# Routed experts of a two-layer network: token rows gathered three groups ahead, target work moved one round later, and eight constant products added to each round

## The reference, cut to what matters

```python
buf = jnp.zeros((E, CAPACITY + 1, H), x.dtype).at[e_flat, slot].set(x[tok])   # E = 64, CAPACITY = 64, H = 128
gu_e = jnp.einsum('ech,ehf->ecf', buf, expert_gate_up_w)
act = _silu(gu_e[..., :I]) * gu_e[..., I:]                                     # I = 64
out_e = jnp.einsum('eci,eih->ech', act, expert_down_w)
y = out_e[e_flat, slot] * w_flat[:, None]
y = jnp.where((pos < CAPACITY)[:, None], y, 0)
y = y.reshape(T, TOP_K, H).sum(axis=1)
```

## Time and profile before

| | before |
|---|---|
| times of 3 runs | 1703.34, 1703.63 (median), 1709.86 us |
| the profiled execution: its time, its span | 1707.66 us, 1704.8 us |
| busy of the span: PE, DVE, ACT, POOL | 88%, 66%, 58%, 54% |
| mean granted clock of TensorE, share of full | 0.941 |
| expert stage: first gather to the end of the span | 1555.9 to 1704.8 us |

### The profile page before, as it was taken

The page is one execution under the profiler, slowest core; times in us unless marked ns, Lnnn a source line. Parts: engine busy times, 40 slices in busy tenths (PEclk is TensorE's granted clock), DMA queues, the critical chain, the costliest instruction groups (busy, mean ns, idle before and its releaser), DMA issues.

```text
span 1704.8 us, 44671 instructions
## 1 busy us (share of the span) xinstructions
PE 1504.1 (88%) x13893; PEld 1081.1 (63%) x13895; DVE 1131.8 (66%) x2702; ACT 989.5 (58%) x2495; POOL 926.9 (54%) x1633
## 2 busy tenths in 40 slices
PE   7989999999999999997999688888888888885786
PEld 5545555555555555545999577777777777774675
DVE  6566555555555555552555598998898998895662
ACT  6445555555555555542334588888888888872342
POOL 6235555555555545545543566666666666632664
PEclk8789999999999999998999699999999999996775
DMA  9132131222222221213332121211211211215442
GB/s 278 36 83 56 48 78 50 55 54 55 57 57 57 57 57 46 54 52 78 65 70 61 28 49 44 46 41 42 46 43 41 45 43 41 45 38 113 87 91 36
DMA packets 240850, 103.36 MB, mean 61 GB/s; under 512 B 145497, under 2 KB 229274, under 8 KB 240794
## 3 DMA queue, kind: packets, MB, share of 16 engines
q1 hardware_dynamic: 230554, 89.04, 22.4%
q0 software_dynamic: 10240, 13.64, 3.7%
HBM read 57.73 MB, written 35.96 MB: 55 GB/s over the span
## 4 chain that ended last, share of the span: by engine, by line
PE 44%; ACT 15%; DMA 11%; DVE 10%; SPq 9%; issue 7%; POOL 4%; POOLq 0%; DVEq 0%; ACTq 0%
DMA remainders<-yT 5%; PE bankA L1883 4%; PE bankB L1929 4%; PE bankT L1912 4%; PE bankT L2068 4%; SPq L370 4%; DMA dq<-remainders 3%; DVE mneg L998 3%; ACT qx L1688 3%; ACT km L1697 2%; ACT gqx L1688 2%; PE bankT L2187 2%; PE bankS L1897 2%; PE bankA L2169 2%; ACT rows L1761 2%
## 5 line engine op out<-in xcount | busy, mean ns | idle before, releaser
L683 POOL TENSOR_SCALAR_AFFINE_SELECT probs<-probs 128x512 f32<-128x512 f32 x256 | 183.4, 739 | 175.0 <-ACT probs L1574 175.0
L1574 ACT ACTIVATE probs<-bankT 128x1024 f32<-128x1024 f32 x128 | 131.1, 1024 | 194.4 <-PE bankT L1915 194.4
L997 DVE TENSOR_REDUCE mneg<-bankS 128x2 f32<-128x256 f32 x256 | 106.6, 416 | 138.1 <-PE bankS L1902 137.4
L998 DVE TENSOR_REDUCE mneg<-bankS 128x2 f32<-128x512 f32 x256 | 174.3, 681 | 0.0
L1912 PE MATMUL bankT<-qT,kT 37*128 37x512 f32 x512 | 139.4, 623 | 11.4 <-ACT probs L1576 6.5
L676 POOL CAST qb<-qT 128x256 bf16<-128x256 f32 x256 | 96.7, 398 | 86.6 <-ACT qT L1569 86.6
L1929 PE MATMUL bankB<-probs,vaug 128*64 128x512 f32 x512 | 142.5, 636 | 1.0 <-ACT yT L1581 1.0
L1883 PE MATMUL bankA<-xnT,wd 128*128 128x256 f32 x480 | 142.1, 409 | 0.0
L1363 DVE STREAM_TRANSPOSE pt<-pe 128x768 f32<-128x768 f32 x128 | 124.4, 972 | 25.2 <-ACT pe L1674 25.2
L1581 ACT COPY yT<-bankB 128x512 f32<-128x512 f32 x128 | 75.1, 587 | 112.9 <-PE bankB L1933 112.9
L1569 ACT ACTIVATE qT<-bankA,bd 128x256 f32<-128x256 f32 x256 | 107.6, 473 | 55.1 <-PE bankA L1883 55.0
(11 more groups left out here) (319 smaller groups left out, 4286.0 us busy)
## 6 DMA issues: line engine op xcount, KB each, us to landing
rzb<-reciprocals SPq DMA_DIRECT2D x128, 128.0 KB, 2.6
yT<-yT SPq DMA_DIRECT2D x64, 128.0 KB, 2.3
xtab<-tab SPq DMA_DIRECT2D x32, 192.0 KB, 2.0
xs_sorted<-zeros SPq DMA_DIRECT2D x1, 4608.0 KB, 19.4
qT<-xs_sorted SPq DMA_DIRECT2D x144, 32.0 KB, 1.8
ys_sorted<-qT SPq DMA_DIRECT2D x36, 128.0 KB, 1.9
value_rows<-vrow SPq DMA_DIRECT2D x32, 128.0 KB, 1.8
vx<-value_rows SPq DMA_DIRECT2D x256, 16.0 KB, 1.8
```

Of the source, the lines that this page charges most:

```text
L683: pool.affine_select(out=blocks, in_=blocks, compare_op=ALU.is_ge, fill=0.0, base=0, pattern=[[0, 4], [1, P]], channel_multiplier=-1).then ...
L998: dve.tensor_reduce(mneg[:, n.half, :, j, 1], bankS[:, :, 128:384], AX.X, ALU.max, negate=True).then_inc(S["red_done"], 1)
L1574: act.activation(pT[:, g % 2].rearrange("p e j t -> p e (j t)"), bankT[:, 0:2, :], ACT.Exp, scale=SCALE0).then_inc(S["exp_done"], 1)
```

## The change

Four things change, all in the expert stage.

- POOL: the gathers of three groups are issued ahead, and in the loop those of group g + 3 are issued ahead of the adds of group g. For g of 2 and more, `fetch_tokens` waits that the gathers of group g - 2, on the same semaphore, have landed.
- DVE: `targets` of group g is no longer at the end of the round of `compare(g)`, but in the round after it, behind `owners1` and ahead of `tokens`.
- PE: `firsts` of group g is likewise in the round after, between `down` and `pick`.
- PE: a new function `fill` issues 8 products at the start of each round from 0 on: `identb` (128 x 128) with `upto` (128 x 256), both bf16, into a part of bank 3 of `bankT` that nobody reads. It waits for nothing.

```diff
+        FILL = 8
+        spare_ps = bankT[:, 3, 0:2 * P]
...
             def fetch_tokens(g):
                 pool.wait_ge(S["sidx_done"], g + 1)
+                if g >= 2:
+                    pool.wait_ge(S[f"xg_in{g % 2}"], 16 * GH * (g // 2))
...
-            fetch_tokens(0)
-            fetch_tokens(1)
+            for g in range(3):
+                fetch_tokens(g)
             for g in range(NG):
-                if g + 2 < NG:
-                    fetch_tokens(g + 2)
+                if g + 3 < NG:
+                    fetch_tokens(g + 3)
                 add_rows(g)
...
             for i in range(-3, NG):
                 if i + 4 < NG:
                     owners1(i + 4)
+                if 0 <= i + 1 < NG:
+                    targets(i + 1)
                 if i + 3 < NG:
                     tokens(i + 3)
                 if 0 <= i + 1 < NG:
                     activate(i + 1)
                 if 0 <= i + 2 < NG:
                     compare(i + 2)
-                    targets(i + 2)
...
+            def fill(count):
+                for k in range(count):
+                    pe.matmul(spare_ps, identb[:, :], upto[:, :, :].rearrange("p k t -> p (k t)"), start=True, stop=True)
...
             for i in range(-3, NG):
+                if i >= 0:
+                    fill(FILL)
                 if 0 <= i + 1 < NG:
                     columns(i + 1)
                 if i >= 0:
                     down(i)
+                if 0 <= i + 1 < NG:
+                    firsts(i + 1)
                 if i + 3 < NG:
                     pick(i + 3)
...
                 if i >= 0:
                     merge(i)
-                if 0 <= i + 2 < NG:
-                    firsts(i + 2)
```

## The result

The changed kernel took 1683.33 us, the median of 4 runs (1676.73 to 1688.38), against 1705.2 us for the kernel before in the same session. The ratio is 0.9865 with a 95% interval of 0.9825 to 0.9906: 16 to 30 us faster; the forecast was 24 us. The profiled execution has a span of 1680.7 us against 1704.8. That these 24.1 us meet the 23.9 of the sum is luck, and the first thing to read is where they lie.

A forecast was written before the change was run, and what follows sets the result against it. The prediction took late gathers, then PE's clock, to bound the kernel. First adds at 1576.2, 77.5 us for 12 intervals and 18.1 for three put the last adds 23.9 us earlier: 1680 us, range 1675 to 1694.

The forecast's parts named there:

- the sum: Expert stage: 12 intervals of 6.46 us plus 18.1 us for the last three; last adds 23.9 us earlier.
- What bounds the kernel: Expert stage: a loop through late gathers, 16.5 us per two groups, sets the pace; PE's clock comes second.
- Gathers three ahead, POOL's queue next: POOL in the expert stage: the gather loop no longer binds; two adds and two gathers set 6.46 us a group.
- the adds' old wait: POOL: adds wait for the group before to land; not binding at median 3.5 us, by some tenths at 5.0 maximum.
- fourth rival: POOL: nothing gained, as adds wait for landings of the adds before; interval 7.8 us, time 1701 us; chance 0.06.
- the prediction's own sign: Expert stage: the forecast would be wrong if adds wait for landings in the middle of the stage.
- `firsts` and `targets` later: DVE and PE: one round later costs 0 to 0.3 us a group; DVE's wait for `firsts` nearly gone.
- the bound: PE's `fill`: 8 products take 0.95 us at full clock, 1.9 at half; clock taken as full nearly throughout.
- First adds and tail: Expert stage: first adds stay at 1576.2, plus or minus 2 us; the last three intervals take 18.1 us.
- The ends given for the case: Whole kernel: 6.42 to 6.7 us a group and first adds 2 us either way give 1676 to 1687 us.
- POOL slowed by a denser DVE: POOL: each of four issues a group takes 0.25 us more, interval 7.46 us, time 1692 us; chance 0.09.
- Slower: PE: clock stays at half, rounds 10.3 us, time 1732 us; decides below 48% of time at full clock; chance 0.06.

The follow-up runs named there:

- two outputs: Changed kernel with odd groups' adds sent to a second array, so adds wait for the landing two groups back: 89.1 us from adds 0 to 15; not timed.
- the repeat: The changed kernel itself, run and profiled once more: ratio 0.9877 to the kernel before, 105.8 us from adds 0 to 15.
- gathers only: Kernel before with gathers three groups ahead and their new wait, `firsts` and `targets` unmoved, without `fill`: ratio 0.9887, 99.9 us from adds 0 to 15.
- no fill: Changed kernel with FILL = 0 instead of 8, all else as changed: ratio 0.9853 to the kernel before, 100.1 us from adds 0 to 15.

## Why the prediction was right, and what in it was not

- *What bounds the kernel.* Right. The loop through late gathers set the pace: the gathers' place alone takes 119.5 to 99.9 us.
- *Gathers three ahead, POOL's queue next.* The mechanism was right and 6.46 us a group is its true floor (two outputs: 77.4 us for twelve), although its own terms, 3.26 + 1.98 + 1.20, add up to 6.44. The size was off: 84.9 and 87.7 us instead of 77.5. The step that failed is the one on the adds' old wait, "not binding at the median, binding at the 5.0 us maximum by some tenths". Two things in it were wrong. The start after a landing, 0.9 us in the fourth rival, was left out: against 4.5 us until the next adds, a landing binds from 3.6 us on (3.6 + 0.92), just above the median, and not from 4.5. Six of the fifteen landings in the trace of before are over that; with the sum's own rows they make 12 intervals of 6.46 us some 4.4 us longer, an estimate that leaves 81.9 us. And the landings were not a fixed spread around 3.5 us, but depend on when the weight loads begin: 3.6 to 5.7 us where one begins near the second add, mostly 3.2 to 3.6 us elsewhere. This was my fourth rival, with a chance of 0.06 and all intervals at 7.8 us; it came true in 6 of the twelve intervals, in the repeat in 9. By the prediction's own sign, adds that wait for landings in the middle of the stage, this part of it was wrong.
- *The new wait in `fetch_tokens`.* Nothing in the profiles points to it, as priced.
- *`firsts` and `targets` later.* Priced at 0 to 0.3 us a group, and I expected DVE's wait for `firsts` nearly gone. It stayed (13.8 us between adds 0 and 12, before 13.2), since `firsts` is behind `fill`, `columns` and `down`, and since DVE, busy 61.0 of 84.9 us, must stand idle somewhere. With gathers three ahead it costs nothing that shows (gathers only 99.9, no fill 100.1); with gathers two ahead it costs 9 us. I had checked what waits behind `firsts`, not what `firsts` itself is queued behind, nor that it left a time in which PE waited anyway.
- *`fill`.* Its length was near: 0.87 us at full and 1.66 at half, from its start to that of `columns` (0.95 and 1.9 by the bound). That 8 products hold the clock was wrong. The clock is 0.90 without them; with gathers two ahead and `fill` it is 0.68. At 8 products it gained nothing in any pair here; with 12 and 16 the clock was 1.00 between adds 0 and 12.
- *First adds and tail.* 21.6 against 20.3 us from first gather to first adds, within the 2 us; the last three intervals 18.2 against 18.1. The ends given for the case, 1676 to 1687 us, are a little wider than its terms (1677 to 1685).
- *POOL slowed by a denser DVE.* Didn't happen. Adds take 1.61 us in the mean where they took 1.63, gathers 1.00 where they took 0.99, with DVE busy 61.0 of 84.9 us:

```profile
L955 POOL DMA_INDIRECT out_x<-ym,aidx x32 | 51.5, 1610 | 23.8 <-ACT ym L1841 10.4 <-issue 7.6 <-DMA out_x<-ym,aidx 5.6
L945 POOL DMA_INDIRECT xg<-xtab,sidx x32 | 32.1, 1002 | 29.6 <-DVE sidx L1511 21.1 <-issue 8.2 <-DMA out_x<-ym,aidx 0.3
```

  What the Trainium skill (SBUF — State Buffer, Who interferes with whom) says of full blocking had no effect on these means. By the same section, a VectorE instruction with two SBUF inputs contends only with a GpSimd instruction that reads SBUF, and descriptor generation, it infers, needs the write interface, which such an instruction doesn't take; my use of it was too wide. The trace agrees with the narrower form: in the kernel before, the three `owners1` comparisons from 1609.26 to 1610.46 took 0.41 to 0.42 us each inside the first add at 1609.15, and that add took 1.63 us.
- *Slower.* Rounds of 10 us in a row came only with `fill` and late gathers together. The point of decision was worked out wrong: rounds of 5.8 and 10.3 us have a mean of 7.96 with 52% of the rounds, which is 38% of the time, at full clock, and not 48%. The clock of 0.68 of that run means 36%.

Against the sum, the profiled stage gained 15.0 us, not 23.9: 16.3 us from adds 0 to 15, less the 1.3 us by which the first adds came later. The second pair of profiles gives 12.2 us from adds 0 to 15. The time was forecast well by luck: its interval is wide (16 to 30 us, the repeat 12 to 30), and the sum's error in the middle, 7.4 us, is less than the four runs differ by (1676.73 to 1688.38).

## What to carry to other kernels

When a queue's in-order waits are relieved, list each wait that stays in the same queue, add the start after it to its price, and ask what else moves while its releaser is under way: here a DMA's landing came late when loads, issued by another engine's progress, began within 1.5 us of it. A median hides that; read the slow cases one by one and look for what stands beside them. A step moved later must be priced by what is now ahead of it in its new place, above all a wait for a DMA, and by whether it leaves a time of waiting for the loop that sets the pace. And products added to hold the clock should be tried without the rest: here they gained nothing at 8 a round, and made each round at half clock 1.66 us longer.

## What the runs showed of the hardware

- The second indirect add of a group, of 128 rows, mostly lands 3.2 to 3.6 us after the start of its issue. It lands 3.6 to 5.7 us after it when the load of a group's weights (256 and 128 KB) begins between 0.6 us ahead of that start and 1.5 us behind it (47 of 47 landings in twelve profiles).
- POOL starts the next adds 0.92 us after the landing that it waited for in the middle of the stage, 0.88 us in its last three groups, in each kernel in which such a wait binds; behind its own previous issue it starts after 0.30 us.
- In both profiles of the changed kernel and in six of the other kernels with gathers three ahead, the adds of group 7 start 1.70 us behind the landing, 0.8 us more than the adds of other groups that waited for one. I don't know why.
- The profile's releaser can mislead here: it names `ym` for the adds at 1618.34, while `ym` of that group was ready at 1610.70 and its own wait was the landing at 1616.64.
